# Gathering the nearest rows while the keys are searched, and looking their factors up by one-hot products

## The chip, the core and the metric

One NeuronCore of a Trainium2 chip runs the whole program. The metric is the device time in microseconds. The engines are TensorE (PE), VectorE (DVE), ScalarE (ACT), GpSimd (POOL) and SyncE (SP), each with its own instruction queue; they meet only at semaphores.

## The reference, cut to what matters

Four graph layers are applied to x (4096 rows of 128 features) with one dense 0/1 matrix adj. Only the last one matters here:

```python
z = leaky_relu(_lap_mul(A, x) @ W1 + b1, negative_slope=0.1)
d2 = sq[:, None] + sq[None, :] - 2.0 * (z @ z.T)
S = jnp.exp(-jnp.sqrt(jnp.maximum(d2, 0.0) + 1e-10) / (2.0 * sigma))
S = jnp.where(ranks < k, S, 0.0)            # k = 4 nearest of each row
A2 = S + A
out = _lap_mul(A2, x) @ W2 + b2             # d[:, None] * (A2 @ (d[:, None] * x)), d = rowsum(A2) ** -0.5
```

So each output row is d_i times (A @ (d x W2) + the sum over its four nearest rows j of S_ij * d_j * (x W2)_j), plus a bias, plus the residual. The factor d_j (the "second-degree factor") of a neighbour is known only when row j itself has been searched.

## The kernel before

Rows are worked in 32 tiles of 128 (P), in 8 groups (NG) of four (G). The program is straight code per engine with counting semaphores; loops over groups are hardware loops (`Fori`), with first and last groups peeled. The order of the work of each engine is the order in the code.

**Key stage** (about 1281 to 1577 us). For each tile TensorE makes 4096 keys per row in eight chunks (`keys`, L818, L819); ScalarE copies each chunk from its bank to a row buffer (L1138), of which there are two, used by tiles in turn; VectorE finds the eight largest keys (L2149, `MAX8`) and then their indices (L2162, `FIND_INDEX8`), after which the buffer is free (`s_keyused`). Between these passes VectorE does the small work of the group before: it keeps the four indices (`distances`, L2115, into TI), takes the similarities (L2121), and makes the factor d (`second_inverse`, L2130; `scaled_rows`, L2134 and L2138), with which it scales the rows of `side` = x W2 into `gsc`. ScalarE stores `gsc` to DRAM (`last_operand`, L1118) and casts it to bf16 (L853); POOL subtracts (`remainder`, L1209), ScalarE casts the rest (`part1`, L857, in the turn of the third tile of a group), POOL subtracts again (`part2`, L1214). These three parts are the operand of the last product. POOL has nothing else in this stage.

**Last stage** (1561 us to the end). TensorE multiplies adj, in panels of one tile each that SP loads from DRAM (L440, four buffers), with the three parts: 32 matmuls of 384 columns per tile into bank q of four (`first_products` for the first group, where all wait for the last parts, then `product`, L681). POOL gathers with an indirect DMA each of the four nearest scaled rows per tile (`last_gathers`, L1431, 128 DMAs of 128 rows of 512 bytes), into buffers for two groups; indices are first copied (`stage_near`, L1422). VectorE sums the three parts out of the bank (`take_product`, L1557), adds the four gathered rows times their similarities (L2222, L2225), and at the end of a group multiplies by d, adds bias and residual (L2228 to L2234). ScalarE stores the output (L1165).

The two row buffers of keys (`rows`), 32 KB per partition, are idle in the last stage, and so are large parts of the space of the earlier layers (`spare`, the weights, the work tiles).

## Time and profile before

| | |
|---|---|
| time of three runs | 1797.57 to 1802.69 us, median 1799.66 |
| the profiled execution | 1797.79 us, its span 1796.1 |
| TensorE busy | 1587.6 us (88% of the span), mean granted clock 0.940 |
| VectorE busy | 1261.5 us (70%) |
| ScalarE, POOL busy | 724.0 us (40%), 587.3 us (33%) |
| key stage, VectorE busy | 99.3 of 100 us |
| DMA | 198.70 MB, mean 111 GB/s |

Busy time is the sum of an engine's instructions. A granted clock of 1.0 is TensorE's upper level (2.4 GHz), 0.5 the lower (1.2 GHz). The profiled execution has one span (first to last instruction) and a device time that is 1.7 us longer; sums of durations from the trace belong to it.

### The profile page before, as it was taken

To read this page: it belongs to the slowest core of one execution; us is meant where nothing else is said; L and a number is where in the kernel's file an instruction comes from. 1 tells how busy PE (TensorE), PEld (TensorE's weight loads), DVE (VectorE), ACT (ScalarE), POOL (GpSimd) and SP (SyncE) were. 2 spreads that over 40 slices of the span, in tenths; PEclk is the share of its full clock that TensorE was granted. 3 is DMA by queue.
4 is the path that set the end of the run, shared out by engine and by line. 5 is a ranking of instruction groups with operands and counts; after the bars stand their busy time and mean duration, and the time that the engine had idled before them with its cause. 6 is when DMAs were issued, how large, how long until landed. Compare 5 with 4: busy or idle time off the path is not lost.

```text
span 1796.1 us, 32841 instructions
## 1 busy us (share of the span) xinstructions
PE 1587.6 (88%) x9151; PEld 928.5 (52%) x9161; DVE 1261.5 (70%) x3487; ACT 724.0 (40%) x1143; POOL 587.3 (33%) x817
## 2 busy tenths in 40 slices
PE   4999999867777778799997999999999999859987
PEld 4777777522333333456664666778544444324544
DVE  7899999856677677646555666642699999933434
ACT  3444444334455555213333222666555555500000
POOL 5333333356655556401110000233000000165663
PEclk8999999977898888899999999999999999978998
DMA  7687787422222222132222222444000000033442
GB/s 246 222 307 283 291 297 288 152 59 70 69 74 73 68 75 75 43 106 93 93 82 83 82 93 87 118 133 124 31 0 6 12 6 6 12 100 126 141 129 72
DMA packets 127159, 198.70 MB, mean 111 GB/s; under 512 B 11859, under 2 KB 96889, under 8 KB 118912
## 3 DMA queue, kind: packets, MB, share of 16 engines
q1 hardware_dynamic: 102592, 172.58, 27.9%
q0 software_dynamic: 11840, 19.18, 3.8%
q10 hardware_dynamic: 12672, 6.29, 1.2%
q8 instruction: 25, 0.41, 0.1%
q14 instruction: 30, 0.25, 0.0%
HBM read 178.13 MB, written 26.21 MB: 114 GB/s over the span
## 4 chain that ended last, share of the span: by engine, by line
PE 66%; DVE 14%; issue 12%; ACT 3%; another core or an unknown queue 3%; DMA 1%; POOL 1%; ACTq 0%; DVEq 0%; POOLq 0%; SPq 0%
PE bank L681 27%; PE bank L606 8%; PE bank L567 7%; PE bank L751 6%; DVE partsA L2149 5%; PE bank L595 4%; PE bank L818 3%; DVE cand L1623 3%; PE bank L530 2%; PE bank L572 2%; PE bank L543 2%; ACT first L919 2%; PE bank L520 1%; PE bank L819 1%
## 5 line engine op out<-in xcount | busy, mean ns | idle before, releaser
L681 PE MATMUL bank<-partsB,panel 128*128 128x387 bf16 (+1 forms) x2048 | 367.2, 338 | 46.2 <-issue 32.7
L681 PEld LDWEIGHTS bank<-partsB,panel 128*128 128x128 fp8e4 x2048 | 204.6, 100 | 204.4 <-issue 65.9
L818 PE MATMUL bank<-wide,partsA 128*128 128x512 f32 x512 | 263.3, 596 | 6.9 <-ACT rows L1138 4.9
L606 PE MATMUL bank<-first,partsB 128*128 128x512 fp8e4 x768 | 238.9, 426 | 5.3 <-issue 5.3
L919 ACT ACTIVATE first<-bank 128x512 fp8e4<-128x512 f32 x256 | 150.4, 597 | 210.1 <-PE bank L595 91.5
L1763 DVE TENSOR_TENSOR gath<-gath,bank 128x512 f32<-128x512 f32 x240 | 162.9, 683 | 102.1 <-PE bank L606 59.7
L1623 DVE MAX8 cand<-bank 128x8 f32<-128x128 f32 x1024 | 216.9, 286 | 10.4 <-PE bank L572 7.8
L567 PE MATMUL bank<-partsA,panel 128*128 128x387 bf16 x1024 | 212.3, 329 | 7.5 <-DVE cand L1623 6.3
L1342 POOL DMA_INDIRECT gath<-pool_features,idx_now x160 | 167.9, 1049 | 84.6 <-issue 57.9
L595 PE MATMUL bank<-panel,tri 128*128 128x512 fp8e4 x256 | 109.5, 430 | 94.5 <-ACT first L919 67.2
L873 ACT ACTIVATE panel<-bank 128x1024 fp8e4<-128x1024 bf16 x128 | 130.9, 1024 | 147.8 <-PE bank L543 147.8
L1557 DVE TENSOR_REDUCE agg<-bank 128x128 f32<-128x384 f32 (+1 forms) x96 | 51.2, 556 | 191.9 <-PE bank L681 110.4
L1138 ACT COPY rows<-bank 128x512 f32<-128x512 f32 x256 | 133.1, 614 | 115.1 <-DVE partsA L2162 86.3
L681 PE MATMUL bank<-partsA,panel 128*128 128x384 bf16 x1024 | 172.4, 327 | 3.4 <-DVE gath L1763 1.7
L1209 POOL TENSOR_TENSOR rem<-gsc,partsB 128x516 f32<-128x516 f32 x23 | 26.0, 1130 | 452.6 <-ACT partsB L853 452.6
L818 PEld LDWEIGHTS bank<-wide,partsA 128*128 128x128 f32 x512 | 95.7, 190 | 103.2 <-ACT rows L1138 55.3
L1431 POOL DMA_INDIRECT gath<-last_features,IDX x128 | 124.2, 970 | 70.7 <-issue 54.0
L681 PEld LDWEIGHTS bank<-partsA,panel 128*128 128x128 fp8e4 x1024 | 99.6, 97 | 71.8 <-DVE gath L1763 2.2
L606 PEld LDWEIGHTS bank<-first,partsB 128*128 128x128 bf16 x768 | 80.7, 107 | 103.2 <-issue 42.4
L2149 DVE MAX8 partsA<-rows 128x8 f32<-128x4096 f32 x28 | 123.6, 4415 | 6.2 <-ACT rows L1138 6.2
L2162 DVE FIND_INDEX8 partsA<-partsA,rows 128x8 uint32<-128x4096 f32 x28 | 123.7, 4420 | 0.3 <-issue 0.3
L567 PEld LDWEIGHTS bank<-partsA,panel 128*128 128x128 fp8e4 x1024 | 89.2, 98 | 45.2 <-issue 10.6
(298 smaller groups left out, 2159.4 us busy)
## 6 DMA issues: line engine op xcount, KB each, us to landing
rows<-in_adj SPq DMA_DIRECT2D x64, 1024.0 KB, 7.0
panel<-adjT_panels SPq DMA_DIRECT2D x96, 512.0 KB
panel<-adjT_panels SPq DMA_DIRECT2D x128, 256.0 KB
adjT_panels<-panel SPq DMA_DIRECT2D x32, 512.0 KB, 3.0
gath<-pool_features,idx_now POOLq DMA_INDIRECT x160
overflow_maxima<-wide POOLq DMA_DIRECT2D x1, 2048.0 KB, 18.3
pool_features<-gsc ACTq DMA_DIRECT2D x8, 256.0 KB, 2.3
rows<-overflow_maxima SPq DMA_DIRECT2D x8, 256.0 KB
```

What stands on the lines that cost most here:

```text
L567: i = pe.matmul(bank[q % 2][:, 0:FW], panel[:, q, j, :], parts_of[0][:, j, :], start=(j == 0), stop=(j == NT - 1))
L595: pe.matmul(tri_bank[j % 2][:, :], tri[:, :], piece[:, j // BPB, :, ts(j % BPB, P)], start=True, stop=True).then_inc(s_tri, 1)
L606: i = pe.matmul(pool_bank[j % 4][:, :], pparts[:, j, k * FE:k * FE + F], first_slot[:, j % SLOTS, :], start=(k == 0), stop=(k == 2))
L681: i = pe.matmul(bank[q][:, 0:3 * w], panel[:, q, j, :], of_block if w < FE else parts_of[u][:, j, :], start=(j == 0), stop=(j == NT - 1))
L818: pe.matmul(o[:, :], zs[:, q % 2, :], zT[:, c * 512:(c + 1) * 512], start=True, stop=False)
L873: act.activation(panel[:, q, c * 8:(c + 1) * 8, :].rearrange("p b i -> p (b i)"), bank[2 + c % 2][:, :].bitcast(BF16), ACT.Copy, saturate= ...
L919: act.activation(first_slot[:, j % SLOTS, :], tri_bank[j % 2][:, :], ACT.Relu, saturate=False).then_inc(s_first, 1)
L1138: act.copy(rows[:, q % 2, c * 512:(c + 1) * 512], bank[c][:, :]).then_inc(s_keyrow, 1)
L1342: pool.indirect_dma_start(main[q][:, k, :], None, feat_dram, bass.IndirectOffsetOnAxis(idx_now[:, q, k:k + 1], axis=0), bounds_check=N - 1 ...
L1623: i = dve.max(cand[:, ch * BPB + b, :], bank[4 + ch % 4][:, b * P:(b + 1) * P])
L1763: dve.tensor_tensor(running[:, j % 2, :], running[:, j % 2, :], pool_bank[j % 4][:, :], ALU.max).then_inc(s_fp_used, 1)
L2149: dve.max(top_v[:, q, :], rows[:, q % 2, :]).then_inc(s_top, 1)
```

## The change

The gathers no longer wait for the scaled rows. The rows of `side`, without d, are stored to DRAM by ScalarE already in the layer before (`store_rows`). POOL gathers the four nearest rows of a tile right after its index search, for the first six groups (`nearest`, into 96 row slots put together from idle space); groups 6 and 7 are gathered in the last stage, 16 DMAs each in a row (`later_nearest`), into the slots of groups 0 and 1. The split of POOL is written out among the gathers: the remainder for group g-2 comes after the gathers of the second tile of group g.

The missing d_j is looked up in the last stage. An index j is taken apart into a column in its tile (j & 127, VectorE, `columns_in_tile`; POOL copies it to bf16, SP stores it to DRAM and loads it back broadcast to all partitions) and the tile. POOL makes a one-hot of the column for 16 neighbours by 128 partitions, and a one-hot of the tile (`one_hots`). TensorE multiplies the column one-hots with d, split into three bf16 parts of 32 tiles (`look_up`: 16 matmuls of 96 columns per group, banks 4 to 7); VectorE multiplies by the tile one-hot, reduces to four factors and multiplies the similarities by them. VectorE's last stage is written out over the groups. The diff, cut to its core:

```diff
+            for g in range(NG - 1):
+                store_columns(g)                       # SP
+            load_columns(0)
+            load_columns(1)
+            store_columns(NG - 1)
+            for g in range(1, NG):
+                turn(g, False)
+                if g + 1 < NG:
+                    load_columns(g + 1)
...
+            def look_up(g, r):                         # TensorE
+                pe.wait_ge(s_hot, g + 1)
+                pe.wait_ge(s_d2p, 4)
+                pe.wait_ge(s_look_used, g * G + 1)
...
+                for q in range(G):
+                    for k in range(TOP):
+                        i = pe.matmul(bank[4 + q][:, k * 3 * NT:(k + 1) * 3 * NT],
+                                      col_hot[r][:, (q * TOP + k) * P:(q * TOP + k + 1) * P],
+                                      d2_parts[:, :, :].rearrange("p k b -> p (k b)"), start=True, stop=True)
+                    i.then_inc(s_look, 1)
+            def last_products(g, r):
+                product(5, g, 0, 3)
+                look_up(g, r)
+                for q in range(1, G):
                     product(5, g, q, 3)
+            look_up(0, 0)
+            last_products(1, 1)
...
+            def store_rows(g):                         # ScalarE, in the layer before
+                act.wait_ge(s_side, NG + g + 2)
+                act.dma_start(side_dram[ds(g * G * P, G * P), :].rearrange("(t p) f -> p t f", p=P),
+                              grp(side, g)).then_inc(s_g2, 16)
...
             def last_operand(g):
-                act.wait_ge(s_gsc, g + 5 * NG + 2)
-                act.dma_start(g2_dram[ds(g * G * P, G * P), :].rearrange("(t p) f -> p t f", p=P),
-                              gsc[:, :, 0:F]).then_inc(s_g2, 16)
                 part0(5, g)
...
-            with pool.Fori(0, NG) as g:
-                split(5, g)
...
+            def nearest(g, q):                         # POOL
+                pool.wait_ge(s_keyused, g * G + q + 1 + 2)
...
                 for k in range(TOP):
+                    pool.indirect_dma_start(near[g * G + q][k], None, side_dram,
+                                            bass.IndirectOffsetOnAxis(top_now[:, q, k:k + 1], axis=0)
+                                            ).then_inc(s_gath2[q], 16)
...
+            for g in range(EARLY_GROUPS):
+                for q in range(G):
+                    nearest(g, q)
+                    if q == 0 and g > 0:
+                        near_columns(g - 1)
+                    if q == 1 and g > 1:
+                        remainder(5, g - 2)
+                    if q == 2 and g > 1:
+                        part2(5, g - 2)
+            near_columns(EARLY_GROUPS - 1)
+            split(5, NG - 4)
+            near_columns(NG - 2)
+            for g in range(NG - 3, NG):
+                split(5, g)
+            near_columns(NG - 1)
...
+            def one_hots(g, r):
+                pool.wait_ge(s_lo[r], 16 * (g // 2 + 1))
+                if g > 1:
+                    pool.wait_ge(s_look, G * (g - 1))
+                pool.tensor_scalar(col_hot[r].rearrange("p (c i) -> p c i", c=NK),
+                                   lo_all[r].rearrange("p (i c) -> p c i", c=NK),
+                                   own_column[:, 0:1], None, ALU.is_equal).then_inc(s_hot, 1)
+                pool.tensor_copy(near_col, columns_of(g)).then_inc(s_tile_hot, 1)
+                pool.tensor_tensor(tile_ge, near_col.unsqueeze(2).to_broadcast([P, NK, NT + 1]),
+                                   tile_start[:, :].unsqueeze(1).to_broadcast([P, NK, NT + 1]), ALU.subtract
+                                   ).then_inc(s_tile_hot, 1)
+                pool.tensor_scalar(tile_ge, tile_ge, 0.0, None, ALU.is_ge).then_inc(s_tile_hot, 1)
+                if g > 1:
+                    pool.wait_ge(s_look_used, G * (g - 1) + 1)
+                pool.tensor_tensor(tile_hot[r], tile_ge[:, :, 0:NT], tile_ge[:, :, 1:NT + 1], ALU.subtract
+                                   ).then_inc(s_tile_hot, 1)
...
+            for g in range(NG):
+                one_hots(g, g % 2)
+                if 2 <= g < 2 + NG - EARLY_GROUPS:
+                    later_nearest(g - 2 + EARLY_GROUPS)
...
+                    if not first_group:                # VectorE, before max_index
+                        dve.wait_ge(s_gath2[q], 16 * TOP * g)
...
+                for q in range(G):                     # VectorE, last(g)
+                    take_product(5, 2 * NT + t, q)
+                    dve.wait_ge(s_look, t + 1)
+                    dve.wait_ge(s_tile_hot, 4 * (g + 1))
+                    dve.tensor_tensor(looked, bank[4 + q][:, 0:TOP * 3 * NT].rearrange("p (c k b) -> p c k b", c=TOP, k=3),
+                                      tile_hot[r][:, q * TOP:(q + 1) * TOP, :].unsqueeze(2).to_broadcast([P, TOP, 3, NT]),
+                                      ALU.mult).then_inc(s_look_used, 1)
+                    dve.tensor_reduce(d2_near[:, q, :], looked.rearrange("p c k b -> p c (k b)"), axis=AX, op=ALU.add
+                                      ).then_inc(s_last, 1)
+                    dve.tensor_tensor(sg[:, q, :], S[:, t, :], d2_near[:, q, :], ALU.mult).then_inc(s_last, 1)
...
+                    for k in range(TOP):
+                        dve.scalar_tensor_tensor(agg[:, q, 0:F], near[t][k], sg[:, q, k:k + 1],
```

Left out are the definitions of the tiles and semaphores, the waits between steps of a chain, two small iotas at the start of the program that make the tile starts and a partition's own column, and `later_nearest`, which waits for the output of group g-6 (`s_fin`) and then issues its 16 gathers.

## Rows read from the trace of the kernel before

**Rows 1.** Stretches: PE, PEld, DVE, ACT, POOL busy (x); clock, DMA, GB/s. Last: L681 alone.

```profile
1400.00:1500.00 100.00, 96.75 (x262) 41.04 (x263) 99.31 (x57) 56.90 (x116) 5.73 (x6) 1.00 0.02 5
...
1588.00:1618.30 30.30, 12.38 (x47) 4.87 (x47) 7.41 (x18) 0.00 (x0) 20.20 (x23) 0.61 0.30 99
...
1644.40:1650.30 5.90, 2.68 (x10) 0.87 (x10) 0.00 (x0) 0.00 (x0) 2.94 (x4) 0.87 0.16 47
...
1588.00:1788.70 200.70, 167.62 (x896) 90.50 (x896) 0.88 0.37 118
```

**Rows 2.** Key stage in order of time, VectorE: start us, length us, instruction.

```profile
1483.39 4.42 DVE L2149 MAX8 partsA<-rows 128x8 f32<-128x4096 f32 x1
...
1488.03 4.42 DVE L2162 FIND_INDEX8 partsA<-partsA,rows 128x8 uint32<-128x4096 f32 x1
1492.37 4.41 DVE L2149 MAX8 partsA<-rows 128x8 f32<-128x4096 f32 x1
```

**Rows 3.** Key stage in order of time, ScalarE and (ACTq) its queue.

```profile
1474.55 4.01 ACT L1138 COPY rows<-bank 128x512 f32<-128x512 f32 x8 [1.97 <-DVE partsA L2162]
1478.38 0.70 ACT L857 CAST partsB<-rem 128x516 f32 x1
1478.90 0.37 ACT L1132 COPY partsA<-wide 128x128 f32 x1
...
1562.36 0.39 ACTq L1118 DMA_DIRECT2D last_features<-gsc  x1
```

**Rows 4.** Last stage in order of time: TensorE's products and POOL's gathers.

```profile
1588.02 7.23 PE L681 MATMUL bank<-partsB,panel 128*128 128x384 bf16 x35 [2.76 <-DMA panel<-adjT_panels]
1597.98 0.48 PE L681 MATMUL bank<-partsB,panel 128*128 128x384 bf16 x1 [1.79 <-issue]
1618.30 26.00 PE L681 MATMUL bank<-partsB,panel 128*128 128x384 bf16 x147 [0.19 <-issue]
...
1578.75 0.99 POOL L1431 DMA_INDIRECT gath<-last_features,IDX  x1 [0.84 <-POOL IDX L1422]
1613.07 0.94 POOL L1431 DMA_INDIRECT gath<-last_features,IDX  x1 [0.30 <-issue]
1620.23 0.95 POOL L1431 DMA_INDIRECT gath<-last_features,IDX  x1 [6.22 <-issue]
1633.03 0.95 POOL L1431 DMA_INDIRECT gath<-last_features,IDX  x1 [3.09 <-DVE agg L1557]
```

**Rows 5.** Last stage in order of time: VectorE's takes of products.

```profile
1618.52 0.56 DVE L1557 TENSOR_REDUCE agg<-bank 128x128 f32<-128x384 f32 x1 [14.36 <-remote]
1783.31 0.56 DVE L1557 TENSOR_REDUCE agg<-bank 128x128 f32<-128x384 f32 x1 [3.73 <-PE bank L681]
1788.61 0.56 DVE L1557 TENSOR_REDUCE agg<-bank 128x128 f32<-128x384 f32 x1 [3.19 <-PE bank L681]
```

**Rows 6.** POOL's compares (groups, one line), and a cast beside VectorE's operations.

```profile
L1286 POOL TENSOR_SCALAR found<-listed 128x16 f32<-128x16 f32 x32 | 8.2, 255 | 114.5 <-DVE listed L1575 114.5
L1311 POOL TENSOR_SCALAR blank_rows_now<-listed 128x64 f32<-128x64 f32 x8 | 3.1, 391 | 0.0
...
L1262 POOL TENSOR_SCALAR found<-cand x32: 317/322/463, 61.4 to 347.3; 128x32 f32<-128x32 f32 x32
...
1206.34 1.90 POOL L1398 CAST adj_ring<-panel 128x2048 fp32r<-128x2048 fp8e4 x1 [4.61 <-PE bank L751]
...
1206.75 0.69 DVE L2080 TENSOR_TENSOR tmp<-bank,DINV 128x512 f32<-128x512 f32 x1 [10.81 <-PE bank L762]
1207.59 1.19 DVE L2084 TENSOR_TENSOR tmp<-tmp,b 128x512 f32<-128x512 f32 x1
...
1271.62 0.69 DVE L2084 TENSOR_TENSOR tmp<-tmp,b 128x512 f32<-128x512 f32 x1
```

**Rows 7.** POOL's subtractions with two inputs: count, min/median/max ns.

```profile
L1209 POOL TENSOR_TENSOR rem<-gsc,partsB x23: 1118/1130/1139, 106.3 to 1574.4; 128x516 f32<-128x516 f32 x23
```

**Rows 8.** TensorE's weight loads, the first layer, eight in a row.

```profile
161.24 0.49 PEld L543 LDWEIGHTS bank<-identb,rows 128*128 128x128 bf16 x8
```

More of the change, by code:

```diff
@@ L97, in program @@
         over_gath = gath[:, 0, MAIN + FIRSTS:MAIN + FIRSTS + OVER, :]
-        near = [gath[:, i // G, (i % G) * TOP:(i % G + 1) * TOP, :] for i in range(2 * G)]
+        near_a = gath[:, :, :, :].rearrange("p a s f -> p (a s) f")
+        near_b = spare[:, 4096:4096 + 4 * G * TOP * F].bitcast(F32).rearrange("p (s f) -> p s f", f=F)
+        EARLY_GROUPS = 6
         over_max = gath[:, 1, MAIN + FIRSTS, :]
@@ L2231, in last @@
                 dve.wait_ge(s_last, c.up())
[L2232 to L2233 removed]
+                if g > 1:
+                    dve.wait_ge(s_out[r], 16 * (g // 2))
                 dve.tensor_tensor(fin[:, r, :, :], grp(X, g), tmp[:, :, :], ALU.add).then_inc(s_last, 1)
                 dve.wait_ge(s_last, c.up())
[L2236 removed]
+                assert c.k == LAST_STEPS, c.k
                 dve.sem_inc(s_fin, 1)
[L2238 to L2242 removed]
+            for g in range(NG):
+                last(g)
 _INS = ['x', 'adj', 'L0_gnn_weight', 'L0_gnn_bias', 'L1_gnn_weight', 'L2_gnn_W', 'L3_gnn_W1', 'L3_gnn_b1',
```

163 lines of the change are left out of this document (105 added, 58 removed).

## The prediction

> **What bounds the kernel now.** A change this late in the program is read backwards from its end, so I began with the stretches by engine [rows 1]. The reader is to see two regimes. From 1281 to 1577 us the keys are made and searched: VectorE is busy 99.4 of 100 us, with one search pass of 4.42 us for the values and one of 4.42 for the indices per tile of 128 rows [rows 1, 2]. From 1561 to 1789 us TensorE makes the last product and VectorE works under half the time. I then read both stages in order of time [rows 2 to 5], and the rows that price the new work [rows 6 to 8].
>
> In the last stage a product (32 matmuls) takes 5.30 us: the last two were taken at 1783.31 and 1788.61 [rows 5]. The 28 products after the first group need 148.4 us and have 200.6 (1588.0 to 1788.6) [rows 1, 5]. Of the 52 us lost, the largest piece is the stretch from 1595.9 to 1618.3: single matmuls 2 to 2.8 us apart, waiting for no semaphore (the first ten of them have one row here) [rows 4]. It begins 17 us into an unbroken run of gathers on POOL (from 1578.75, one each 1.25 us, to 1614.0) and ends some 2 to 4 us after it [rows 4]. A run of 12 (from 1633.0 to 1648.3) gives the same from 1644.5 to 1650.2, 10 matmuls in 5.9 us; between the two, 147 go through in 26.0 us [rows 1, 4]. The granted clock, 1.00 in the key stage, is a mean of 0.61 from 1588.0 to 1618.3: most of that stretch stands at the lower of the two levels (1.2 GHz) [rows 1]. So the gathers' length of run, not their data, hurts TensorE.
>
> **What the change does, part by part.**
>
> *Key stage: gathers of four per tile.* POOL now gathers after each tile's index search, in runs of 4 with some 4 us between; no such run slows TensorE in the rows of before, so nothing for the gathers themselves. But POOL's remainder for group g-2 is moved behind the gathers of the second tile of group g. Who waits? ScalarE, for its second part, and ScalarE also copies the key rows. Worked from the end of that tile's index search (call it E): POOL needs 1.0 us to start (from a take's end at 1619.08 to the gather at 1620.23 it is 1.15 [rows 4, 5]), 4.7 for four gathers, 1.13 for the remainder [rows 7]; ScalarE 0.7 for its cast, 0.3 for the staging of z, 4.0 for eight copies [rows 3]. VectorE can start the next values at E + 12.0. It would have been ready at E + 9.0 (1483.39 to 1492.37 [rows 2]): now 3.0 us late. The remainder is in this place in groups 2 to 5 only: 4 x 3.0 = 12.0 us. The bounds are 0 (POOL's gathers overlapping more than I think) and 4 x 4.5, if TensorE's clock falls in its idle stretch and the next keys come late too. Cover lost elsewhere: none; the part is still made a group early.
>
> *Key stage: VectorE's own additions.* A wait on the gather semaphore stands between the two searches, after the wait for the first one, so it is exposed: one sequencer step, about 0.11 (the 0.22 from 1487.81 to 1488.03 hold one such step and a short load [rows 2]), for 24 tiles: 2.6. The mask of the columns is one small operation and a wait (as the gap just named, and the smallest row of its kind [rows 2, 6]), 0.25 x 7 = 1.8. The removed wait for the store ran under a search: nothing. Key stage: 12.0 + 2.6 + 1.8 = **+16.4**.
>
> *Earlier and at the start.* Two small iotas before the constants are ready: 0.3 (each under POOL's smallest compare, 0.255 [rows 6]). Eight stores of rows issued from ScalarE's queue, 0.4 each [rows 3], in a stretch where TensorE is the busy engine; I take 0.5 for the last one, by the widening (bounds 0 and 3.2). Taking the store out before the last operand gives 0.4 back, since TensorE waits for that part. Column stores and loads go on SP's queue: the eight stores make it wait while it has nothing else to load, and each load of columns stands behind four panel loads of a group that have 16 us to land: nothing, unless SP is held by a late one-hot.
>
> *Last stage, TensorE.* 16 weight loads with short matmuls per group: eight loads of that size took 0.49 us [rows 8], so 0.9 and 0.1 for waits, 1.0. The first look-up fits into TensorE's wait for the panel (2.8 us [rows 4]); seven more count.
>
> *Last stage, POOL.* Per group one compare of 2048 elements with a 32-byte step, and four small operations (16, 528, 528, 512 elements). The trace has no such compare. From below, the cast of 2048 elements: 1.9 us [rows 6]. Compares of 16 and 64 elements took 0.255 and 0.391, 2.8 ns for each further element, 5.9 for 2048; a strided one of 32 took 0.322, 4.1 ns an element more than the first, and this is the end above: 8.6 us [rows 6]. A long operation with two inputs costs 1.13 for 516, 2.2 ns each, 4.5 for 2048 [rows 7]. I take 5.0, between the long one and the compares' slope. The rest 0.3 + 1.15 + 1.4 + 1.13 and four waits, 4.4. First look-up operands ready at 1578.4 + 9.5 = 1587.9.
>
> *POOL against VectorE.* An add with both inputs in SBUF took 1.19 us beside POOL's cast and ended 0.54 after it; alone it takes 0.69; one with an input in PSUM took 0.69 in the middle of the same cast [rows 6]. So VectorE's accumulations (two inputs in SBUF) stop while POOL computes. I carry this from 1.9 to 5 us of POOL work. The Trainium skill (SBUF — State Buffer, SBUF: two separate sides) states an exclusive lock held for the full instruction; by that rule the trace agrees, and the row stretched to 5 us stays as taken. Without such blocking the sum would be 13.5 us lower.
>
> VectorE per tile: take 0.58, products of the look-up 0.57, reduction 0.6, one small and four accumulations 0.2 + 4 x 0.38 = 1.7: 3.5 us. TensorE's second look-up waits until VectorE has taken the four look-ups of group 0: 1587.9 + three tiles (10.4) + 1.15 = 1599.4, plus POOL's compares for groups 1 and 2 (10.0) and 3.5 of the small ones, 1612.9. TensorE has been ready since 1593.3: **19.6 us lost**. Then 1.0 + 3 x 5.3 + 6 x (21.2 + 1.0) brings it to 1763.0. The two late groups are gathered in runs of 16, 20 us each. By the runs above, TensorE crawls from about 14 us into a run to 2 after it, 8 us, and gets a sixth of its work done: 6.7 x 2 = 13.3. Half clock after these and after the long wait: 3. End 1779.3 against 1788.6: -9.3. Behind it, two more operations in the tail, +1.3 (0.57 and 0.6, with gaps), and the -0.4: last stage **-8.4**.
>
> **Sum**: 16.4 + 0.8 - 8.4 = +8.8 us. The profiled execution took 1797.8 (span 1796.1), so 1806.6; the median of the three runs shown is 1.9 above the profiled one: **1808**.
>
> **Rivals.**
> 1. *Cheap one-hots, not slower.* The place is POOL from 1578 us, the price the cast's 1.9 us instead of 5.0 [rows 6]. Each us there counts for about 3.5 in TensorE's first wait (once in the start, twice in the blocking, and the small compare goes along): -11, total -2, time 1797. It decides below 3.5 us. For it: the cast moves as many bytes at 0.93 ns an element [rows 6]. Against it: every compare row is dearer per element. The Trainium skill (GPSIMD Engine Reference, Engine selection) states that one-input work there runs at roughly line rate, which would be this case; no row here shows a long compare.
> 2. *Runs of 16 do no harm.* If the crawl needs the 28 in a row, or the wait for VectorE, and not the run alone: -14.8, 1794. Against it: all five runs of 11 or 12 gathers end in a crawl, of which one is shown [rows 1, 4]; for it, the runs of 8 do not.
> 3. *Dear one-hots.* At 8.6 us TensorE's first wait grows by 14, and POOL's 13.5 a group cannot lie beside VectorE's 8.4 with two inputs: 21.9, all of TensorE's 22.2, so that most of the two runs' 40 us of POOL, some 16, comes on top. +30, 1838.
> 4. *No stall in the key stage*, because ScalarE's part finds its remainder in time: -12, 1796. Only a faster start of the gathers would do it.
> 5. The gathers moved but POOL's queue delays them, so that VectorE's index search waits: the gather of a tile has 37 us until its buffer of indices is rewritten; hardly.
>
> **How the numbers follow.** A measurement of this kernel tells about 0.3% (5.4 us) from no change, so same is 1794.3 to 1805.1. Forecast 0.43 (own range 1799 to 1820), rival 1 0.18, rival 2 0.14, rival 3 0.14, rival 4 0.09, rival 5 or a change that misses its aim 0.02. Faster: half of rivals 1, 2 and 4 (they lie at the bound) and the low end of the forecast with one of them, 0.27. Same: 0.18. Slower: 0.55. The range 1786 to 1834 leaves out combinations of rivals 1 and 2 below and the full price of rival 3 above.
>
> **What would show it.** Key stage: in groups 2 to 5 ScalarE's cast of the second part ends some 12 us after its row copy, and VectorE idles about 3 us before the fourth tile's values; VectorE's last index search ends near 1594 instead of 1577. Last stage: gaps between TensorE's first and second product of group 1 of some 20 us; accumulations that end with POOL's compare; two crawls, inside the two runs of 16. The prediction is wrong if the compare lasts under 3.5 us, if VectorE shows no idle time in the key stage, or if no crawl follows the runs.

## The result, and the profile after

The changed kernel takes 1806.83 us (median of seven runs, 1803.14 to 1810.07) against 1799.66 for the kernel before in the same comparison (1796.27 to 1802.69): a ratio of 1.0043, 95% interval 1.0028 to 1.0057. It is slower by 7.2 us, where 8.3 were forecast (1808 less 1799.66). One execution of a version below (one-hots on ScalarE, remainder early, late gathers in runs of 16) took 2034.04 us at a mean granted clock of 0.745 and is left out of its time.

The profiled execution took 1810.07 us (span 1808.4), the slowest of the seven, and stands 12.3 us above the profiled one of before. The whole difference, by three marks of each trace (first values search, end of the last index search, last matmul):

| us | before | after | difference | forecast |
|---|---|---|---|---|
| start to first search of the key stage | 1281.9 | 1286.8 | +4.9 | +0.8 |
| key stage | 295.6 | 307.4 | +11.8 | +16.4 |
| last index search to last matmul | 211.1 | 205.5 | -5.6 | -9.3, and -0.4 |
| tail behind the last matmul | 7.5 | 8.7 | +1.2 | +1.3 |
| span | 1796.1 | 1808.4 | +12.3 | +8.8 |

The stretches of after answer to [rows 1] (columns as there: PE, PEld, DVE, ACT, POOL busy; clock, DMA, GB/s):

```profile
1386.00:1486.00 100.00, 92.56 (x246) 40.61 (x250) 91.50 (x58) 60.02 (x118) 44.12 (x47) 0.97 0.10 26
...
1608.00:1627.00 19.00, 1.09 (x11) 0.66 (x10) 18.26 (x25) 0.00 (x0) 18.47 (x9) 0.58 0.08 28
...
1645.00:1656.00 11.00, 3.82 (x13) 1.16 (x12) 2.04 (x7) 0.00 (x0) 5.70 (x7) 0.66 0.27 90
...
1684.00:1697.00 13.00, 6.08 (x16) 1.33 (x17) 0.59 (x2) 0.00 (x0) 10.71 (x9) 0.58 0.25 67
```

VectorE, 99.31 of 100 us busy in the key stage before, is at 91.50. In the last stage TensorE stands still for 18 us in one place and crawls in two. (A crawl is a stretch in which matmuls go out singly, 0.7 to 2.8 us apart, where they otherwise follow each other every 0.166 us.)

**The stall in the key stage**, answering to [rows 2, 3]. In order of time, after, one tile (the third of a group) and what follows it:

```profile
1378.10 4.42 DVE L2277 MAX8 partsA<-rows 128x8 f32<-128x4096 f32 x1
...
1378.95 0.96 POOL L1512 DMA_INDIRECT gath<-last_rows,partsA  x1 [4.12 <-DVE partsA L2292]
...
1382.72 0.95 POOL L1512 DMA_INDIRECT gath<-last_rows,partsA  x1 [0.30 <-issue]
...
1383.69 1.13 POOL L1301 TENSOR_TENSOR rem<-gsc,partsB 128x516 f32<-128x516 f32 x1
1384.94 0.63 ACT L940 CAST partsB<-rem 128x516 f32 x1 [11.70 <-POOL rem L1301]
1385.47 0.29 ACT L1220 COPY partsA<-wide 128x128 f32 x1
1385.67 3.99 ACT L1226 COPY rows<-bank 128x512 f32<-128x512 f32 x8
...
1389.81 4.43 DVE L2277 MAX8 partsA<-rows 128x8 f32<-128x4096 f32 x1 [2.62 <-ACT rows L1226]
```

It is the chain of the prediction: gathers, remainder, cast, row copy, search. ScalarE waits 11.70 us for the remainder, the fourth tile's keys are copied late, and VectorE's next search for values starts 11.71 us after the last one, where 1483.39 to 1492.37 [rows 2] is 8.98. The same step takes 11.68 to 11.71 us in all four groups.

**The last stage**, groups by line, after (busy, mean ns of one, idle before):

```profile
L1556 POOL TENSOR_SCALAR rows<-rows,own_column 128x2048 bf16<-128x2048 bf16 x8 | 59.0, 7381 | 40.5 <-issue 32.5 <-DMA rows<-nearest_columns 7.8
...
L2387 DVE TENSOR_TENSOR partsA<-X,tmp 128x512 f32<-128x512 f32 x8 | 16.2, 2021 | 0.3
L2370 DVE TENSOR_TENSOR sg<-partsA,d_near 128x4 f32<-128x4 f32 x32 | 16.1, 503 | 1.1
...
L896 PE MATMUL bank<-rest,rows 128*128 128x96 bf16 x128 | 7.6, 215 | 22.2 <-DVE rows L2363 17.9 <-POOL rows L1556 3.1 <-issue 1.2
L896 PEld LDWEIGHTS bank<-rest,rows 128*128 128x128 bf16 x128 | 6.8, 103 | 22.7 <-issue 21.8
```

The compare (L1556) takes 7.38 us. The look-ups (L896) waited 17.9 us for VectorE, once. The same place in order of time shows who held VectorE:

```profile
1606.53 0.56 DVE L2363 TENSOR_TENSOR rows<-bank,rows 128x384 f32<-128x384 f32 x1 [5.39 <-POOL rows L1570]
1607.12 0.55 DVE L2367 TENSOR_REDUCE d_near<-rows 128x4 f32<-128x384 f32 x1
1607.71 4.43 DVE L2370 TENSOR_TENSOR sg<-partsA,d_near 128x4 f32<-128x4 f32 x1
...
1606.53 7.32 POOL L1556 TENSOR_SCALAR rows<-rows,own_column 128x2048 bf16<-128x2048 bf16 x1
...
1626.53 0.72 PE L896 MATMUL bank<-rest,rows 128*128 128x96 bf16 x7 [17.91 <-DVE rows L2363]
```

The multiplication of four numbers per row (L2370) has both inputs in SBUF and lasted 4.43 us, inside POOL's compare; the operation with an input in PSUM (L2363) and the one with one input (L2367) ran beside the same compare in 0.56 and 0.55. It ended at 1612.14, 1.7 us before the compare's recorded end (1613.85), and the four accumulations after it took 1.51 us, 0.38 each.

**The crawl**, answering to [rows 4]. After, the first gather of the first run of 16 (the last ends at 1652.5), and TensorE within it, in order of time:

```profile
1632.69 1.03 POOL L1547 DMA_INDIRECT gath<-last_rows,partsA  x1 [3.20 <-DVEq L2390]
...
1648.39 0.32 PE L742 MATMUL bank<-partsB,panel 128*128 128x384 bf16 x1 [1.79 <-issue]
1650.49 0.48 PE L742 MATMUL bank<-partsB,panel 128*128 128x384 bf16 x1 [1.78 <-issue]
```

Single matmuls, some 2 us apart, waiting for nothing that the profile shows, as in the kernel before.

### The profile page after: what moved, and what is told of

It reads as the page before. It is cut to its first block, busy times and chain, and to the rows that moved or that the text cites. A ratio compares the mean times of both kernels' runs of the same rounds, so it can differ in the third digit from the quotient of the medians.

```text
span 1808.4 us, 32982 instructions
## 1 busy us (share of the span) xinstructions
PE 1585.7 (88%) x9279; PEld 934.6 (52%) x9289; DVE 1342.0 (74%) x3587; ACT 727.7 (40%) x1143; POOL 674.0 (37%) x859
## 4 chain that ended last, share of the span: by engine, by line
PE 70%; DVE 13%; issue 7%; another core or an unknown queue 3%; ACT 3%; POOL 2%; DMA 0%; DVEq 0%; ACTq 0%; POOLq 0%; SPq 0%
PE bank L742 25%; PE bank L667 9%; PE bank L879 8%; PE bank L628 7%; PE bank L812 6%; PE bank L656 4%; DVE cand L1747 3%; PE bank L633 2%; PE bank L591 2%; PE bank L604 2%; PE bank L880 2%; DVE partsA L2277 1%; ACT first L1002 1%; DVE partsA L2292 1%
## 5 line engine op out<-in xcount | busy, mean ns | idle before, releaser
L742 PE MATMUL bank<-partsB,panel 128*128 128x387 bf16 (+1 forms) x2048 | 357.7, 334 | 21.6 <-issue 12.9
L879 PE MATMUL bank<-wide,partsA 128*128 128x512 f32 x512 | 266.0, 601 | 19.2 <-ACT rows L1226 17.8
L956 ACT ACTIVATE panel<-bank 128x1024 fp8e4<-128x1024 bf16 x128 | 130.9, 1024 | 147.7 <-PE bank L604 147.7
L742 PE MATMUL bank<-partsA,panel 128*128 128x384 bf16 x1024 | 172.4, 327 | 3.5 <-DMA panel<-adjT_panels 1.7
L1226 ACT COPY rows<-bank 128x512 f32<-128x512 f32 x256 | 137.1, 600 | 84.3 <-DVE partsA L2292 36.8
L656 PEld LDWEIGHTS bank<-panel,tri 128*128 128x128 bf16 x256 | 26.5, 104 | 161.5 <-issue 143.6
```

The lines of the kernel that those rows point to most:

```text
L656: pe.matmul(tri_bank[j % 2][:, :], tri[:, :], piece[:, j // BPB, :, ts(j % BPB, P)], start=True, stop=True).then_inc(s_tri, 1)
L742: i = pe.matmul(bank[q][:, 0:3 * w], panel[:, q, j, :], of_block if w < FE else parts_of[u][:, j, :], start=(j == 0), stop=(j == NT - 1))
L879: pe.matmul(o[:, :], zs[:, q % 2, :], zT[:, c * 512:(c + 1) * 512], start=True, stop=False)
L1226: act.copy(rows[:, q % 2, c * 512:(c + 1) * 512], bank[c][:, :]).then_inc(s_keyrow, 1)
```

## The experiments

Each group of runs was made on one chip, beside the kernel before on that chip. Chips B to E are four different ones; which one A was is not on record, so A may be E, seen at another time. They differ, and this came to be the main finding:

| | kernel before there, us | runs |
|---|---|---|
| chip A | 1799.66 | the result above |
| chip B | 1720.46 | first four edits |
| chip C | 1720.14 | before and after again, two combinations |
| chip D | 1721.39 | contiguous one-hots, later look-up, no look-up |
| chip E | 1787.35 | later look-up again |

Each group was also made at one time, so "chip" below stands for chip and time together. Times of edits are compared as ratios to the kernel before on their chip, or by stretches of their traces. "Last stage" below is from the end of the last index search to the end of the last matmul. The expectations of the first four runs were written with chip A in view.

### The remainder one tile earlier

```diff
-                    if q == 1 and g > 1:
+                    if q == 0 and g > 1:
                         remainder(5, g - 2)
-                    if q == 2 and g > 1:
+                    if q == 1 and g > 1:
                         part2(5, g - 2)
```

> The changed kernel, with POOL's remainder and second part for group g-2 moved one tile forward: behind the gathers of the first and the second tile instead of the second and the third. My theory (ScalarE is held by the remainder and copies the fourth tile's keys late): the step from the third to the fourth values search in groups 2 to 5 falls from 11.7 us to 9.0, the last index search ends 10.9 us earlier, and the total falls by 10 to 12 us against the changed kernel. Rival (the gathers themselves disturb VectorE or ScalarE, or TensorE's clock falls): the 11.7 us stay, and the total with them.

Measured: 1748.77 us, ratio 1.0161 (1.0136 to 1.0187). In order of time, VectorE, third and fourth tile of a group in this trace:

```profile
1342.26 4.42 DVE L2277 MAX8 partsA<-rows 128x8 f32<-128x4096 f32 x1
...
1351.27 4.41 DVE L2277 MAX8 partsA<-rows 128x8 f32<-128x4096 f32 x1
```

The step is 9.01 us again, in all four groups, and the key stage 296.6 us: 10.8 less than with the stall (307.4 on every chip), and 1.0 more than before. The stall is the remainder behind the second tile's gathers, and VectorE's own additions (24 waits, 7 masks) cost 1.0 us together, not the 4.4 of the sum. The total could not be read against chip A: the ratio lay far above the 1.0043 there, although a cost had been removed. Against the changed kernel on chip C (1757.34, below) it is 8.6 us less, where 10 to 12 were expected.

### The late gathers in runs of 8

```diff
-                if 2 <= g < 2 + NG - EARLY_GROUPS:
-                    later_nearest(g - 2 + EARLY_GROUPS)
+                if 2 <= g < 6:
+                    later_nearest(EARLY_GROUPS + (g - 2) // 2, (0, 1) if g % 2 == 0 else (2, 3))
```

> The changed kernel, with the 32 late gathers issued as four runs of 8, one behind each of POOL's one-hots for groups 2 to 5, instead of two runs of 16. My theory (it is the length of a run of gathers that makes TensorE crawl): no stretch of matmuls 0.7 to 2 us apart is left (in the changed kernel 1645 to 1655 and 1684 to 1697 us), and the total falls by 12 to 20 us. Rival (the crawl comes from the gathers' traffic against the panel loads, however they are cut): as many us of crawl, spread over four places, and a total within 4 us of the changed kernel.

Measured: 1750.87 us, ratio 1.0189 (1.0168 to 1.0210). The trace has no crawl, but neither has the one of the edit above, with its two runs of 16. As a test of the crawl the pair says nothing here. It shows something else: TensorE's waits in the last stage, by line and what ended them, with runs of 16 (first fence, the edit above) and with runs of 8:

```profile
PE bank L896 <- DVE rows L2363: 25.3, 2, 17.9
```

```profile
PE bank L896 <- DVE rows L2363: 16.5, 1, 16.5
```

The second wait, 7.4 us, is gone, and the last stage is 181.5 us instead of 192.4. The edit above differs by its early remainder too; the changed kernel itself, on chip C, has the same second wait (6.3 us) and a last stage of 191.5, so the runs of 8 are worth 10 us of it. While POOL issues 16 gathers, 20 us, the next one-hots stand in its queue, and TensorE comes to need them. On chip A there is no such wait; that the crawl had held TensorE up for as long is the likely reason, and not shown. The total is 6.5 us under the changed kernel on chip C; the 12 to 20 expected counted on a crawl to remove.

### Half the column compare

```diff
-                                      col_hot[r][:, (q * TOP + k) * P:(q * TOP + k + 1) * P],
+                                      col_hot[r][:, (q % 2 * TOP + k) * P:(q % 2 * TOP + k + 1) * P],
...
-                pool.tensor_scalar(col_hot[r].rearrange("p (c i) -> p c i", c=NK),
-                                   lo_all[r].rearrange("p (i c) -> p c i", c=NK),
+                pool.tensor_scalar(col_hot[r].rearrange("p (c i) -> p c i", c=NK)[:, 0:NK // 2, :],
+                                   lo_all[r].rearrange("p (i c) -> p c i", c=NK)[:, 0:NK // 2, :],
```

Left out: the one-hots of the third and fourth tile of each group; their look-ups (first hunk, TensorE) use those of the first and second, so the factors are those of other rows.

> The changed kernel, with POOL's long compare made for 8 of the 16 neighbours of a group; the look-ups of the third and fourth tile use the one-hots of the first and second, so their factors are those of other rows (that part of the computation is left out). The compare falls from 7.4 to about 3.8 us. My theory (it delays the first look-up once, and blocks VectorE's operations with two inputs in SBUF twice more): TensorE's wait before its second look-up falls from 18.2 us by about 3 x 3.6 to 7 us, and the total falls by 10 to 16 us. Rival (the compare is only late, it does not block VectorE): the wait falls by 3.6 us, and the total by about as much.

Measured: 1739.48 us, ratio 1.0120 (1.0100 to 1.0139). The compare of 1024 elements takes 3.99 us (7.38 for 2048: 3.3 ns for each further element, with little that is fixed). TensorE's wait for VectorE before the second look-up is 9.5 us instead of 17.9, the later wait is gone too, and the last stage is 172.4 instead of 191.5. A compare that is 3.4 us shorter took 8.4 off the first wait: between the rival's once and the theory's three times, and so the rival (the compare is only late) has fallen. The total is 17.9 us under the changed kernel on chip C, a little more than the 10 to 16 expected.

### The column one-hots on ScalarE

```diff
-                pool.tensor_scalar(col_hot[r].rearrange("p (c i) -> p c i", c=NK),
-                                   lo_all[r].rearrange("p (i c) -> p c i", c=NK),
-                                   own_column[:, 0:1], None, ALU.is_equal).then_inc(s_hot, 1)
+                act.activation(col_hot[r].rearrange("p (c i) -> p c i", c=NK),
+                               lo_all[r].rearrange("p (i c) -> p c i", c=NK),
+                               ACT.Abs, bias=own_column[:, 0:1]).then_inc(s_away, 1)
+                act.wait_ge(s_away, g + 1)
+                act.activation(col_hot[r], col_hot[r], ACT.Relu, bias=ones_col[:, 0:1], scale=-1.0).then_inc(s_hot, 1)
```

(The lines taken out are POOL's, those put in ScalarE's. own_column holds the negative; the passes make |column - own| and then the positive part of 1 less that. Not shown: ScalarE makes the one-hots two groups ahead, between its output stores.)

> The changed kernel, with the column one-hots made on ScalarE, which is idle in the last stage: the absolute value of (column - partition), then relu(1 - that), in place of POOL's compare. POOL keeps the four small operations, about 4.1 us a group. If ScalarE's two passes take 1.9 us each, as its copies of that size suggest: TensorE's wait before the second look-up falls from 18.2 to below 6 us; VectorE's accumulations, 0.41 us each on the mean beside POOL now, fall towards 0.36; the total falls by 14 to 22 us, the two crawls staying. Rival (VectorE's own longer work per tile is what TensorE waits for): the wait stays above 12 us.

Measured: 1735.44 us, ratio 1.0090 (1.0069 to 1.0111). Groups by line in the last stage of this trace (busy, mean ns of one, idle before):

```profile
L1255 ACT ACTIVATE rows<-rows,own_column 128x2048 bf16<-128x2048 bf16 x8 | 32.2, 4022 | 87.6 <-DMA rows<-nearest_columns 71.5 <-DVEq L2398 16.1
...
L2395 DVE TENSOR_TENSOR partsA<-X,tmp 128x512 f32<-128x512 f32 x8 | 5.5, 692 | 0.3
```

The strided pass takes 4.02 us on ScalarE and the contiguous one 2.00, together less than POOL's one of 7.38, on an engine that has nothing else to do. VectorE's last addition of a group is back at its 0.69 us, from 2.02. TensorE's wait is down to 4.8, the last stage to 167.0. So TensorE's first wait is 17.9 us with the whole compare on POOL, 9.5 with half of it and 4.8 with none. The rival, a wait above 12 us, has fallen; the total is 21.9 us under the changed kernel on chip C, at the upper end of the 14 to 22 expected.

### Both kernels again, on a chip without the crawl

> The kernel before, unchanged, so that its trace can be laid beside those of the edits. On the chip of the first four edits it took 1720.5 us, 79 less than on the chip of the first comparison, and none of the four edits' traces has the crawl of single matmuls. Theory (the crawl belongs to the chip, not to the kernel): where the whole takes some 1720, no two matmuls of one product stand over 1 us apart from 1545 us to the end although the run of 28 gathers is there, the key stage lasts the same 295.6 us, the last stage (last index search to last product) some 170 instead of 211, and the pooling stage (350 to 750 us) is shorter as well. Rival (the crawl is the kernel's and the 79 us are elsewhere, as in a faster key stage or transfers): the crawl is there within the run of 28, the last stage lasts 211. If this comes out at 1800 again, it is the first chip's kind and the crawl must be there.

> The changed kernel, unchanged. Theory (crawl by chip): on a chip without the crawl the shorter runs buy nothing, and the change costs its key-stage stalls (10.9 us), the wait before the second look-up (18 us), a further wait at some later look-up, since TensorE is no longer held up as much as POOL is (7 us in the edit with the early remainder), and 8 look-ups of 1 us: 1755 to 1761, ratio 1.020 to 1.024; no matmul gaps over 1 us inside the two runs of 16. Rival (the chip scales all alike, and the four edits' ratios of 1.009 to 1.019 are what the edits cost): ratio 1.004, 1728. On a chip of the first kind: 1807, ratio 1.004.

Measured: before 1720.57 us (ratio 1.000); after 1757.34, ratio 1.0209 (1.0180 to 1.0239). The same stretch of TensorE in the kernel before as [rows 1] has it, on chip C: from 1557.9 to 1706.4, all 28 products.

```profile
1557.90:1706.40 148.50, 148.49 (x896) 87.22 (x896) 73.05 (x178) 0.00 (x0) 114.12 (x124) 1.00 0.50 156
```

896 matmuls in 148.5 us, where they took 200.7 on chip A. In this trace all 128 gathers make one unbroken run, 1549.8 to 1712.8, and there is no crawl in it. The last stage is 157.9 us against 211.1 (53.2 less; some 170 were expected), and the key stage the same 295.6. The first search starts at 1252.9 against 1281.9 (29.0 less), and the tail is 7.4 longer: together the 74.8 us between the spans. The theory held: the crawl comes with the chip and the run of gathers together, and not with the run alone. After came out within its 1755 to 1761.

So the change had bought, on chip A, relief from a disturbance that chip C does not have. In the last stage it costs 33.6 us on chip C (191.5 against 157.9). On chip A the kernel before is longer there by 53.2 us (211.1 against 157.9) and after by 14.0 (205.5 against 191.5): the crawl took 39.2 us less from it, and 33.6 less 39.2 is the -5.6 of chip A. The stall is the same on both, and so is TensorE's first wait; the later waits, 6.5 us together, are only on chip C. In the last stage of after there:

```profile
PE bank L896 <- DVE rows L2363: 24.4, 3, 17.9
PE bank L896 <- POOL rows L1556: 3.1, 1, 3.1
```

One more thing decides how much the moved gathers are worth. On chip C the tail behind the last matmul of the kernel before is 14.9 us instead of 7.5. In order of time:

```profile
1709.35 0.94 POOL L1431 DMA_INDIRECT gath<-last_features,IDX  x1 [0.30 <-issue]
...
1714.40 1.13 DVE L2222 SCALAR_TENSOR_TENSOR agg<-gath,sg,agg 128x128 f32<-128x128 f32 x3 [3.01 <-DMA gath<-last_features,IDX]
```

VectorE waits for gathers there, and 128 of them at 1.27 us each outlast TensorE: POOL's queue sets the end. (The fence shows one of POOL's last gathers, and VectorE's wait for the last.)

### All three edits, and two of them

> The three edits together: remainder one tile earlier, column one-hots on ScalarE, late gathers in runs of 8. Theory (the costs are separate and add): the last stage of the edit on ScalarE (175.6 us from the last index search), less 10.9 for the stalls; on a chip without crawl 1724 (ratio 1.002), the same as with runs of 16, since there is no crawl to break; on a chip with it some 1800.0 - 17, 1783 (ratio 0.991), and 10 or more below the version with runs of 16. Rival (ScalarE's 6 us passes, in the last stage alone, do not interact with the early remainder but POOL's shorter runs let its small operations fall upon VectorE more often): 1730 without crawl.

> Remainder one tile earlier and column one-hots on ScalarE; the late gathers stay in runs of 16. Theory: without crawl 1724, as the version with runs of 8 (within 3 us of it); on a chip with the crawl two crawls of 6.7 us each stay, 1796 (ratio 0.998), against 1783 for runs of 8. Rival (runs of 16 do no harm, and the crawl only seemed tied to them): the two versions agree on a chip with the crawl as well.

Measured: 1727.58 us, ratio 1.0040 (1.0025 to 1.0055), with runs of 8; 1727.72, ratio 1.0046 (1.0032 to 1.0059), with runs of 16. The two agree, as the theory had it for a chip without crawl, and both lie some 4 us above its 1724. Simple addition missed that the last stage grows when the stall goes: it is 169.9 and 170.6 us against 167.0 with the one-hots on ScalarE alone. Of this, 0.6 and 1.4 us are TensorE's wait before the second look-up (5.4 and 6.2 against 4.8); the rest is not taken apart. That wait is the largest one left.

### The one-hots contiguous

```diff
-                pool.tensor_scalar(col_hot[r].rearrange("p (c i) -> p c i", c=NK),
-                                   lo_all[r].rearrange("p (i c) -> p c i", c=NK),
+                pool.tensor_scalar(col_hot[r], lo_all[r],
                                    own_column[:, 0:1], None, ALU.is_equal).then_inc(s_hot, 1)
...
-                                      col_hot[r][:, (q * TOP + k) * P:(q * TOP + k + 1) * P],
+                                      col_hot[r].rearrange("p (i c) -> p c i", c=NK)[:, q * TOP + k, :],
```

> The changed kernel with the column one-hots compared and written in the order in which the columns lie, so both sides of the compare step by 2 bytes; TensorE then loads its look-up weights with a step of 32 bytes. Rival theory of the prediction, cheap one-hots (it is the 32-byte step that made 7.35 us of 2048 elements; contiguous, POOL runs at the cast's 0.93 ns an element): compare 1.9 to 2.5 us, TensorE's wait before the second look-up 18 less about 2 x 5, the second wait gone, some 15 us less than the changed kernel on the same chip (1757 on the last chip: 1742). Own theory (the compare itself costs some 2.9 ns an element on POOL, as the 528 contiguous elements in 1.54 us do): 5.9 to 6.2 us, waits 3 us shorter, total some 3 to 6 us less (1752). The weight loads with a step may cost more than 103 ns: 128 of them, under 0.1 us each, is at most 10 us against either.

Measured: 1745.99 us, ratio 1.0144 (1.0127 to 1.0161), from 1.0209. POOL's compare and TensorE's loads of the look-up weights in this trace:

```profile
L1556 POOL TENSOR_SCALAR rows<-rows,own_column 128x2048 bf16<-128x2048 bf16 x8 | 43.9, 5483 | 24.8 <-issue 24.4
...
L896 PEld LDWEIGHTS bank<-rest,rows 128*128 128x128 bf16 x128 | 9.4, 160 | 16.4 <-issue 15.8
```

5.48 us: the step of 32 bytes is 1.9 us of the 7.38, and the compare itself is the rest. It is three times the cast's price for as many elements [rows 6], so cheap one-hots were never to be had on POOL. It lies below my 5.9 too. The total did not follow my theory: it fell by 11.3 us (from 1757.34), where I had 3 to 6 and the rival 15, because the later wait went, as the rival had it. The weight loads went from 103 to 160 ns, 7 us over 128 of them, and yet the last stage fell from 191.5 to 178.7, since the compare counts more than once in TensorE's waits (13.8 us left of the 17.9, and the later waits gone). The two last stages are of chips C and D; the kernel before takes the same on both within 0.1%.

### The second look-up later

To all three edits this is added:

```diff
-                product(5, g, 0, 3)
-                look_up(g, r)
-                for q in range(1, G):
+                first = isinstance(g, int)
+                for q in range(G):
                     product(5, g, q, 3)
+                    if q == (2 if first else 0):
+                        look_up(g, r)
```

(`g` is an integer in the peeled group 1 alone.)

> The three edits together (1727.6 on a chip without crawl, before 1720.1), and the look-up of group 1 put behind that group's third product instead of its first. Theory (what is left of TensorE's wait in the last stage, 5.8 us before the second look-up, is the wait for VectorE to take the look-ups of group 0, and TensorE has two products that do not need them): the gap goes, 1722 (ratio 1.001). Rival (VectorE is as late with the products as with the look-ups, since both stand in its one order of work; TensorE then waits before the second or third product instead): 1727. On a chip with the crawl of single matmuls: theory 1778 to 1785 (before 1800), no crawl in runs of 8; if runs of 8 crawl as well, 1790.

Measured: 1720.26 us, ratio 0.9993 (0.9982 to 1.0004). TensorE's waits from the end of the key stage on, in this trace:

```profile
PE bank L743 <- DMA panel<-adjT_panels: 0.7, 1, 0.7
PE bank L897 <- DVE rows L2372: 0.6, 1, 0.6
```

The wait is gone, not moved, and the rival's 1727 has fallen with it. The last stage is 162.1 us, 7.8 less than with the three edits alone.

### No look-up

Left out: the column loads, the one-hots, the look-up matmuls, and with them the neighbour's second-degree factor (VectorE multiplies the similarity by itself in its place). The remainder is one tile earlier.

> The changed kernel with the remainder one tile earlier, and with the look-up left out whole: no column loads, no one-hots, no look-up matmuls, and VectorE scales by the similarity alone (left out: the second-degree factor of the neighbour). It bounds what moving the gathers can bring. On the last chip the kernel before had TensorE full (20.0 of 20) through its last stage, but its 128 gathers made one unbroken run to 1712.8, 6 us after the last product, and the end came 8.5 us after the last gather. Theory (the gathers set the end there, TensorE stands 7 us behind it): 1720 - 7 + 1 of VectorE's mask and waits = 1714, ratio 0.996. Rival (moving the gathers is worth nothing at all without the crawl): 1720 or more. On a chip with the crawl: the 52 us of lost matmul time go but for two crawls of 6.7: some 1765, ratio 0.98.

Measured: 1714.76 us, ratio 0.9958 (0.9942 to 0.9974). The last stage is 156.7 us and the tail 7.5, against 157.9 and 14.9 of the kernel before on chip C: TensorE gained 1.2 us and the tail 7.4, and the key stage took 1.1. So 6.6 us is about what this way of moving the gathers can bring on a chip without crawl, because the queue of gathers no longer outlasts TensorE. The look-ups with their waits removed (162.1 and a tail of 8.5) cost 5.4 us of it in the last stage, and 1.0 in the tail.

### The later look-up on one more chip

> The kernel of the run before (remainder early, one-hots on ScalarE, runs of 8, second look-up later), once more and against the kernel before, to see it on one more chip. If it is a chip without the crawl of single matmuls: before 1720, this 1720, ratio 0.998 to 1.000. If it is one of the first kind (before 1800): theory (runs of 8 do not crawl, and all of the last stage's 52 us of lost matmul time goes) last stage 162 instead of 211, key stage +1, ratio 0.972 to 0.980, some 1752 to 1763; rival (the crawl comes with any 32 gathers in 60 us) ratio 0.99, 1780 or more.

Measured: 1742.07 us against 1787.35, ratio 0.9728 (0.9698 to 0.9757). This chip is of the first kind: the key stage begins at 1278.2 and the granted clock from 350 to 750 us is 0.84, as on chip A. The stretch of the trace from TensorE's first product of group 1 to its last matmul:

```profile
1582.20:1736.70 154.50, 153.65 (x1008) 91.67 (x1007) 114.78 (x265) 38.86 (x14) 56.05 (x58) 1.00 0.43 136
```

1008 matmuls without a crawl (no two stand over 0.72 us apart), at full clock. The ratio came out as the theory had it; its 1752 to 1763 us did not, since this chip's kernel before takes 1787 and not 1800. The last stage is 161.9 us, the same as on chip D (162.1), while the gathers run in eights. The kernel before was not traced on chip E; its time, less the 1.7 us around the span, a start of 1278.2, a key stage of 295.6 and a tail of 7.5, leaves about 204 for its last stage, near the 211.1 of chip A. That it crawls there is worked out so, and not seen. This version beats the kernel before by 2.7% on chip E and equals it on chip D; the changed kernel was not run on chip E.

## Why the prediction was right, and which of its steps were not

The forecast, 1808, and its sign came out, and the mechanisms it named are in the trace. That it came within 1.2 us is partly luck: the key stage cost 4.6 us less than forecast and the last stage with its tail gained 4.0 less, and the two cancel. It was luck, too, that the comparison fell on a chip with the crawl. Step by step:

- **Key-stage stall, 4 x 3.0 forecast: right.** Measured 4 x 2.7 (steps of some 11.70 against 8.98; the terms of the prediction's own chain add up to E + 11.8, not 12.0, and 2.8 was nearer), in groups 2 to 5 and in no other. Undoing the one move gave 10.8 us back. Rival 4 has fallen: ScalarE did not find its remainder in time.
- **VectorE's own additions, 4.4 forecast: too high.** 1.0 us, by the key stage without the stall (296.6 against 295.6). The sequencer step of 0.11 us per wait and 0.25 per mask were mostly covered by the wait that stood there already.
- **Start and earlier layers, +0.8: 0.2 of it seen.** On both chips after runs 0.1 to 0.2 us behind from the start on, which fits the iotas. The rest of the +4.9 on chip A comes between 350 and 1000 us, most of it before 750, where the granted clock was 0.82 after and 0.84 before. It is no fixed cost of the change: on chip C the first search starts at 1252.9 before and at 1252.6 after, and over all traces of chips B, C and D between 1247.6 and 1253.2.
- **The compare, 5.0 us (1.9 to 8.6): mis-sized.** 7.38. I took a value between the long two-input operation and the slope of the small compares; it was nearer to the strided compare of [rows 6].
- **TensorE's wait before the second look-up, 19.6 us: near, by two errors against each other.** It was 17.9 us (1608.6 to 1626.5). From the moment when the first operands stood ready the forecast had 25.0 us (1587.9 to 1612.9) and the trace has 20.1 (1606.4 to 1626.5), in spite of the longer compare. I had laid POOL's time wholly on top of VectorE's. In the trace a compare costs VectorE only what is left of it when VectorE comes to an operation with two SBUF inputs: 4.3 us (4.43 less 0.16) of the first, 3.7 of the second; the takes and reductions before that run on.
- **The lock: right.** Rows 6 showed it for a cast of 1.9 us and it carried over to 7.4. On ScalarE the same one-hots leave VectorE's addition at 0.69 us. The Trainium skill (SBUF — State Buffer, SBUF: two separate sides) states that whichever of POOL's operation and a VectorE operation with two SBUF inputs (or in a two-port mode) starts first gets the shared ports for the whole instruction, and the other fully blocks; the trace agrees on which operations are stopped (4.43 us for L2370; 0.56 for L2363 and 0.55 for L2367), but not quite on the length: VectorE's operation ends 1.7 us before the compare's recorded end. By the skill's rule it would be held 6.1 us there, and by the trace 4.4; the recorded ends on POOL are rough, so which is off stays open.
- **Two crawls, 13.3 us: right in place, too small.** 29 matmuls in the 24 us of the two stretches, at 0.166 each (5.30 for 32) 19.2 us lost. By the last stages of chips A and C the crawl cost after only 14.0 us net, since on C the later waits come in its place. Rival 2 (runs of 16 harmless) has fallen on chip A. On chip C runs of 16 do no harm, but there the kernel before has no crawl to lose either, so the rival's premise, 52 us of lost time, is gone with it.
- **Rival 1, cheap one-hots, has fallen for good.** Even contiguous the compare costs 5.48 us. The Trainium skill (GPSIMD Engine Reference, Engine selection) has one-input work there at roughly line rate; the cast's 0.93 ns an element would fit that, the compare's 2.7 contiguous and 3.6 strided do not.
- **Rival 3, dear one-hots.** The price, 7.4, came nearer to its 8.6 than to mine. What it said of the consequence, that POOL's work would become the bound of every group, did not come on chip A: POOL's last-stage arithmetic blocks VectorE for less than its length. A weak form of it are the later waits on chip C, 6.5 us, behind a run of 16.

What no step had was the question whether the crawl would be there at all. One trace, of one chip, had it, and the forecast treated it as a property of the program. By its own third sign, "if no crawl follows the runs", it is right on chip A and wrong on chip C. On chip C the change is 2.1% slower, five times as much as on chip A; scaled to the forecast's 1799.66 that is 1837, above its range.

Open: what makes the chips differ, or whether it is the chip or the time at which it ran. In both kinds the instructions are the same and the gathers take 1.25 us each; the crawling matmuls wait for nothing recorded. It was not tried whether the kernel before with its gathers in eights loses its crawl on chip A; that the length of the run matters is read from the two traces of chip A and from the one of chip E, and no pair of runs on one such chip shows it.

## What to carry to other kernels

A piece of work moved to another engine's queue is priced by what then stands behind it: the remainder moved by one tile cost 10.9 us and cost nothing one tile earlier, and a look-up moved by two products took 7.8 us off the last stage (169.9 to 162.1). Work given to POOL should have its price measured per operation and layout, and be laid against VectorE's operations with two SBUF inputs; an idle ScalarE did it in less time and blocked nobody. And when the gain of a change is a disturbance that goes away, ask first on how many chips the disturbance exists; the version that was worth having removed its own costs and so won 2.7% on a chip of the slower kind and lost nothing on one of the faster.

## What was not expected of the hardware

- The same program takes 1720 to 1721 us on three chips, 1787 on a fourth and 1800 on chip A. The traces of the kernel before on chips A and C run equal to 350 us, stand 29.5 us apart by 750, and 29.0 from there to the end of the key stage. In the first of these stretches TensorE's mean granted clock is 0.84 on chip A and 0.93 on chip C (0.82 to 0.84 in the three traces of A and E, 0.92 to 0.94 in the eleven of B, C and D). The rest comes in the last stage, where single matmuls stand 2 us apart during long runs of gathers on chip A, and never do on chip C, even in a run of 128.

```profile
350.00:750.00 400.00, 297.62 (x1265) 130.65 (x1266) 270.81 (x601) 188.81 (x328) 236.92 (x240) 0.84 0.25 71
```

```profile
350.00:750.00 400.00, 310.82 (x1439) 135.41 (x1440) 285.23 (x649) 192.05 (x335) 234.92 (x240) 0.93 0.27 76
```

(The kernel before on chip A, and on chip C.)

- A small operation can be the dearest: four numbers per row, 0.16 us when free, 4.43 us when it meets a compare on POOL. And what is stopped ends before the compare's recorded end, at each length of compare. After, the first compare of the last stage, and the same place with the contiguous one:

```profile
1595.02 7.33 POOL L1556 TENSOR_SCALAR rows<-rows,own_column 128x2048 bf16<-128x2048 bf16 x1
...
1595.26 5.41 DVE L2349 TENSOR_TENSOR rest<-rest 128x32 bf16<-128x32 f32 x1
```

```profile
1557.69 5.46 POOL L1556 TENSOR_SCALAR rows<-rows,own_column 128x2048 bf16<-128x2048 bf16 x1
1557.93 3.54 DVE L2348 TENSOR_TENSOR rest<-rest 128x32 bf16<-128x32 f32 x1
```

VectorE is done 1.7 us before the end in both (1600.67 of 1602.35, 1561.47 of 1563.15). The same operation takes 0.19 us where POOL is idle.

- POOL's compare in bf16: 2.7 ns an element contiguous, 3.6 with a step of 32 bytes. TensorE's load of 128 bf16 weights: 103 ns contiguous, 160 with a step of 32 bytes. ScalarE: 2.00 us for 2048 elements contiguous, 4.02 strided.
